# A spectral tokenizer and a transformer block: the first pass's order, the last pass rewritten with four banks for fc1, and head rows that are not turned

## The chip, the cores and the metric

The kernel runs on one core of a Trainium2 chip. All data are 32-bit floats. The metric is the device time of one execution in microseconds; the median of three runs is given. The profile is of one more execution.

## The reference, cut to what matters

For 128 images of 64x64 pixels with 3 channels a Fourier network with 32 channels makes one number per pixel; the 64x64 numbers of an image are then 64 tokens of width 64 for one transformer block.

```python
h = layer_norm(x @ fc0_w + fc0_b, ln0_g, ln0_b)
for i in range(4):
    h = spectral_conv(h, w1, w2) + conv(h) + conv_b[i]      # 24 x 12 modes are kept
    h = layer_norm(h, ln_g[i], ln_b[i])
    if i < 3: h = gelu(h)
h = gelu(h @ fc1_w + fc1_b)          # 32 -> 128
h = gelu(h @ fc2_w + fc2_b)          # 128 -> 64
h = h @ fc3_w + fc3_b                # 64 -> 1, "the head"
h = concatenate([cls_tok, h])        # 65 tokens of width 64
h = h + state_space_scan(layernorm(h))
h = h + (attention, then 8 experts of which 2 are chosen)(layernorm(h))
```

## The kernel before, in words

The program has two parts, `build_tokenizer` and `build_block`, one after the other with a barrier between. In each part every engine has a program of its own, in an order written by hand, and engines meet at counting semaphores.

**Tokenizer.** It makes five passes over the images, and between two passes mixes the Fourier modes of a layer. A pass takes two images (a pair) per step, 64 steps, in a loop that does two steps a turn (`p` is 0 or 1, which buffer). A step handles 4 chunks `j` of 512 columns. The chunk numbers run through all passes; `g0` is the first chunk of the step, and `behind(...)` names the chunk that a stage works on `lag` chunks later, so one step holds the front of its own pair and the back of the one before.

- In a pass PE forms a chunk in a bank `H` (first pass: `inverse_y`, L313, from the turned image `image_t`; later passes: `conv` plus `inverse_y`), ACT squares it (`squares`), DVE sums the squares (`variance`), POOL raises to the power -1/2 (`pool_step`, L683), and DVE multiplies (`normal`; in the first four passes three operations, with gain and shift). ACT then writes the chunk twice (`gelus`, L383 and L387), PE turns it to channels (`to_channels`, L325), ACT copies that out (`channels_out`, L393), and `forward_x` (L337) and `forward_y` (L347) make the spectrum. `pe_mid`, `act_mid` and `dve_mid` are the programs of the first four passes.
- First and middle passes had the same order before: chunks go in twos (`inverse_y(0)`, `inverse_y(1)`, later 2 and 3; the same for `squares` and `variance`).
- The last pass (`pe_last`, `act_last`, `dve_last`) has the three dense layers in place of the spectrum. The activations lie as 4 row groups of 32 channels; `fc1` (`dense1_of`, L524) multiplies each group with a 32x128 weight. Two matmuls go to the banks `M[0]` and `M[1]`, ACT reads them with a GELU (L600), and then the other two go to the same banks. `fc2` (`dense2_of`, L531) writes two halves of `TP`, then two of `H[3]`, which ACT reads (L606). `fc3` (`dense3_of`, L543) takes two chunks and writes 4 column groups of `H[2]`; DVE copies it (L648), PE turns the copy with 4 transposes (`turn_heads`, L551), DVE adds the bias and picks columns (L658), and SP stores 64 numbers per partition (L252). Gain and shift of the last norm are applied by ACT while it copies from the turned bank `TC` (L593). The spectrum's first inverse step, `inverse_x` (L480), writes `M[0]` and `M[1]`, and ACT copies each to `v_sb` (L613).

**Block.** 16 groups of 8 images. `scan_phase(g, g-1)` runs the scan of a group beside the experts of the one before, `attention_phase(g)` follows. SP loads the tokens of a group into `rows` (L1291) when the group before has turned its own; PE turns them with 4 matmuls (L1382), DVE copies the result to `h_in` (L1645) and puts the class token beside it (L1647), and the first norm begins (`mean` on PE, L1339, then `cen` on DVE, L1581).

## Time and profile before

| | |
|---|---|
| median of 3 runs | 9224.98 us (9206.96 to 9254.56) |
| the profiled execution's own time | 9221.47 us |
| its span | 9219.4 us |
| busy: PE, DVE, ACT, POOL | 7821.1 (85%), 4927.3 (53%), 5171.0 (56%), 4060.8 (44%) us |
| granted TensorE clock, mean over the span | 0.898 |

### The profile page before, as it was taken

How to read it: one execution, taken by the hardware profiler on the slowest of the kernel's cores; microseconds unless marked ns; L12 is line 12 of the kernel's file. 1: busy time of each engine (PE TensorE's matmuls, PEld its weight loads, DVE VectorE, ACT ScalarE, POOL GpSimd, SP SyncE). 2: the span in 40 equal slices, each digit the busy share in tenths (PEclk: the TensorE clock that was granted, in tenths of full speed). 3: DMA queues.
4: the chain of work that ended last, by engine and by line, in shares of the span. 5: the costliest groups of instructions: out<-in, count | busy, mean ns of one | idle time of the engine just before them, and what ended most of it. 6: DMA issues, size and time to landing. Idle time of an engine off the chain costs nothing. (4 is left out here: it accounts for less than half of the span.)

```text
span 9219.4 us, 151061 instructions
## 1 busy us (share of the span) xinstructions
PE 7821.1 (85%) x50544; PEld 5411.4 (59%) x50544; DVE 4927.3 (53%) x8481; ACT 5171.0 (56%) x8851; POOL 4060.8 (44%) x1780
## 2 busy tenths in 40 slices
PE   7778789998899988999889999999967676767767
PEld 4555467776677766777654444444436455555555
DVE  5666657776577765777622222222245555555554
ACT  5676657776577765777656666666632222121212
POOL 6676537776377763777523333333321111111110
PEclk7887799999999989999999999999978787878787
DMA  1121244444444444444431111111100000000000
GB/s 67 75 79 74 83 164 160 154 157 137 169 158 150 158 136 173 153 157 157 142 112 38 38 38 42 38 38 38 38 31 2 2 2 2 2 1 2 1 2 1
DMA packets 569388, 730.82 MB, mean 79 GB/s; under 512 B 451944, under 2 KB 490984, under 8 KB 503656
## 3 DMA queue, kind: packets, MB, share of 16 engines
q1 hardware_dynamic: 569320, 729.87, 24.0%
q8 instruction: 48, 0.79, 0.0%
q14 instruction: 20, 0.16, 0.0%
HBM read 375.30 MB, written 354.45 MB: 79 GB/s over the span
## 5 line engine op out<-in xcount | busy, mean ns | idle before, releaser
L683 POOL TENSOR_TENSOR sb_rstd<-sb_var,sb_minus_half 128x16 f32<-128x16 f32 x1280 | 3697.4, 2903 | 3052.9 <-DVE sb_var L427 1599.3
L337 PEld LDWEIGHTS M<-sb_table,sb_pix 128*128 128x128 f32 x8192 | 1024.9, 206 | 196.3 <-ACT sb_pix L387 132.9
L387 ACT ACTIVATE sb_pix<-sb_unit 128x512 f32<-128x512 f32 x1024 | 1101.8, 1076 | 0.0
L434 DVE TENSOR_TENSOR sb_unit<-H,sb_rstd 128x512 f32<-128x512 f32 x1024 | 703.0, 687 | 682.9 <-POOL sb_rstd L683 677.5
L337 PE MATMUL M<-sb_table,sb_pix 128*128 128x52 f32 x8192 | 1041.2, 289 | 0.0
L383 ACT ACTIVATE sb_act_px<-sb_unit 128x512 f32<-128x512 f32 x1024 | 646.9, 632 | 582.0 <-DVE sb_unit L440 581.3
L325 PE MATMUL TC<-sb_table,sb_act_px 128*128 128x128 f32 x4096 | 688.2, 294 | 227.3 <-ACT sb_act_out L393 114.3
L1812 POOL TENSOR_TENSOR blk_dB<-blk_dB,blk_dB 128x260 f32<-128x260 f32 x256 | 187.4, 735 | 1462.3 <-DVE blk_dB L1672 1457.1
L427 DVE TENSOR_REDUCE sb_var<-sb_square 128x16 f32<-128x528 f32 x1024 | 672.2, 696 | 287.8 <-ACT sb_square L376 287.7
L304 PE MATMUL H<-sb_conv_block,sb_act_in 128*128 128x128 f32 x6144 | 780.6, 281 | 0.0
L325 PEld LDWEIGHTS TC<-sb_table,sb_act_px 128*128 128x128 f32 x4096 | 499.4, 154 | 461.8 <-issue 334.2
L304 PEld LDWEIGHTS H<-sb_conv_block,sb_act_in 128*128 128x128 f32 x6144 | 727.4, 194 | 38.6 <-issue 24.6
L600 ACT ACTIVATE sb_dense<-M,sb_fc_bias 128x512 f32<-128x512 f32 x1024 | 647.4, 683 | 178.5 <-PE M L524 178.5
L437 DVE TENSOR_TENSOR sb_unit<-sb_unit,sb_gain_row 128x512 f32<-128x512 f32 x1024 | 708.5, 692 | 35.1
L440 DVE TENSOR_TENSOR sb_unit<-sb_unit,sb_shift_row 128x512 f32<-128x512 f32 x1024 | 708.5, 692 | 34.9
L376 ACT ACTIVATE sb_square<-H 128x512 f32<-128x512 f32 x1024 | 562.0, 594 | 233.7 <-PE H L318 124.2
L524 PE MATMUL M<-sb_act_out,sb_fc_rep 32*128 32x512 f32 x2048 | 677.1, 640 | 3.2 <-ACT sb_dense L600 2.3
L393 ACT ACTIVATE sb_act_out<-TC 128x512 f32<-128x512 f32 x1024 | 611.4, 597 | 44.8 <-PE TC L325 43.9
L1514 ACT ACTIVATE blk_silu<-bank 114x260 f32<-114x260 f32 x384 | 148.7, 387 | 858.6 <-PE bank L1356 856.4
L636 DVE TENSOR_REDUCE sb_var<-sb_square 128x16 f32<-128x528 f32 x256 | 179.9, 703 | 740.8 <-ACT sb_square L587 740.8
L1396 PE MATMUL bank<-blk_bc,blk_select 128*128 128x260 f32 x1536 | 446.2, 406 | 113.6 <-DVE blk_dB L1686 85.3
L524 PEld LDWEIGHTS M<-sb_act_out,sb_fc_rep 32*128 32x128 f32 x2048 | 226.4, 183 | 440.8 <-ACT sb_dense L600 207.7
(231 smaller groups left out, 12102.2 us busy)
## 6 DMA issues: line engine op xcount, KB each, us to landing
act_scratch<-sb_act_out SPq DMA_DIRECT2D x256, 1024.0 KB, 3.9
sb_act_in<-act_scratch SPq DMA_DIRECT2D x256, 1024.0 KB, 5.3
spectrum_in<-sb_f_sb SPq DMA_DIRECT2D x512, 78.0 KB, 1.8
sb_x_in<-spectrum_in SPq DMA_DIRECT2D x48, 832.0 KB, 4.2
spectrum_out<-sb_y_sb SPq DMA_DIRECT2D x48, 832.0 KB, 4.4
sb_z_in<-spectrum_out SPq DMA_DIRECT2D x512, 78.0 KB, 5.1
sb_w_raw<-in_w_mix_dram SPq DMA_DIRECT2D x48, 208.0 KB, 4.0
sb_image_in<-in_x_dram SPq DMA_DIRECT2D x64, 96.0 KB, 2.0
```

What stands on the lines that cost most here:

```text
L304: e.matmul(H[j][:, 128 * u:128 * u + 128], act_in[p][:, 128 * b:128 * b + 128], conv_block[:, :], start=(u == 0), stop=False, skip_group_c ...
L325: mm = e.transpose(TC[:, 128 * u:128 * u + 128], act_px[k % 2][:, 128 * u:128 * u + 128], const("ident"))
L337: mm = e.matmul(M[u][:, 52 * g:52 * g + 52], pix[1 - p][:, at:at + 128], const("f1"), start=True, stop=True)
L383: e.activation(act_px[k % 2][:, :], unit[k % 2][:, :], gelu).then_inc(px_ready, 1)
L387: e.activation(dst, unit[k % 2][:, :].rearrange("p (x c) -> p c x", c=16), gelu).then_inc(pix_ready, 1)
L427: e.tensor_reduce(var[j][:, :], square[j % 2][:, :].rearrange("p (y c) -> p y c", c=C + 1), AX.X, ALU.add).then_inc(var_ready, 1)
L434: e.tensor_tensor(rows, H[k][:, :].rearrange("p (y c) -> p y c", c=C), rstd[k][:, :].unsqueeze(2).to_broadcast([128, 16, C]), ALU.mult).th ...
L437: e.tensor_tensor(rows, rows, gain_row[:, :].unsqueeze(1).to_broadcast([128, 16, C]), ALU.mult).then_inc(scaled, 1)
L440: e.tensor_tensor(rows, rows, shift_row[:, :].unsqueeze(1).to_broadcast([128, 16, C]), ALU.add).then_inc(affine_ready, 1)
L524: e.matmul(M[v][:, :], fc1_rep[at:at + 32, :], act_out[q][at:at + 32, 512 * k:512 * k + 512], start=True, stop=True).then_inc(fc1_done, 1)
L600: e.activation(dense1[2 * w + v][:, :], M[v][:, :], ACT.Gelu, bias=fc1_bias[:, 0:1], scale=1.0).then_inc(fc1_act, 1)
L683: e.tensor_tensor(rstd[j][:, :], var[j][:, :], minus_half[:, :], ALU.pow).then_inc(rstd_ready, 1)
```

## The change

- First pass only: PE, ACT and DVE take the chunks one at a time. `inverse_y(j+1)` stands behind each `to_channels`, `squares(j+1)` and `gelus` alternate, and DVE alternates `variance` and `normal`. The middle passes keep their order.
- Last pass: new programs for PE, ACT and DVE. `fc1` writes four banks (`M[0]`, `M[1]`, `TP`, `H[3]`) from its four row groups at once; `fc2` then writes two of them. `inverse_x` uses `H[2]`, one half after the other, in turn with `fc3`. Gain and shift are folded into `fc1` ahead of the pass (`fc1_scaled`, `fc1_shifted`), and DVE, not ACT, copies `TC` out. `turn_heads` and the two small DVE operations go: DVE adds the bias as it copies `H[2]` to `head_rows`, and SP stores rows of 512 numbers, 4 DMAs per pair in place of 1.
- Block: since the heads now lie in DRAM image by image, 32 DMAs per group write `h_in` itself, 4 partitions each. The loads of group `g+1` are issued once `h1` of group `g` is there. The turning matmuls and both DVE copies go; the class token is written once.

```diff
-                e.dma_start(heads[n], head[p][:, :]).then_inc(st_h[p], 16)
+                for half in range(2):
+                    e.wait_ge(head_ready, 2 * n + half + 1)
+                    for v in range(2):
+                        e.dma_start(heads[n][half, v], head_rows[half][v:128:32, :]).then_inc(st_h[half], 16)
                 return
...
                 if front and not first and j % 2 == 0:
                     conv(j)
                     conv(j + 1)
+                if front and first and j == 0:
+                    inverse_y(0)
                 if three:
                     to_channels(*three)
-                if front and j % 2 == 0:
+                if front and first and j < 3:
+                    inverse_y(j + 1)
+                if front and not first and j % 2 == 0:
                     inverse_y(j)
                     inverse_y(j + 1)
...
             for j in range(4):
                 two, three = (behind(g0, p, j, lag, front, back) for lag in (2, 3))
-                if two and j == 0:
+                if front and first and j == 0:
+                    squares(0)
+                if two and (first or j == 0):
                     gelus(*two)
                 if three:
                     channels_out(*three)
-                if front and j % 2 == 0:
+                if front and first and j < 3:
+                    squares(j + 1)
+                if front and not first and j % 2 == 0:
                     squares(j)
                     squares(j + 1)
-                if two and j > 0:
+                if two and not first and j > 0:
                     gelus(*two)
...
+            if first:
+                for j in range(4):
+                    if front:
+                        variance(j)
+                    if front and j > 0:
+                        normal(g0 + j - 1, j - 1)
+                    if back and j == 0:
+                        normal(g0 - 1, 3)
+                if back:
+                    spectrum()
+                return
...
+        FC1 = (M[0], M[1], TP, H[3])
...
+            def dense1_of(c, q, k):
+                e.wait_ge(act_ready, c + 1)
+                at_least(e, fc2_act, 2 * (c - HEAD0))
+                for r in range(4):
+                    e.matmul(FC1[r][:, :], fc1_scaled[32 * r:32 * r + 32, :],
+                             act_out[q][32 * r:32 * r + 32, 512 * k:512 * k + 512],
                              start=True, stop=True).then_inc(fc1_done, 1)
+            def dense2_of(c):
+                for w in range(2):
+                    e.wait_ge(fc1_act, 4 * (c - HEAD0) + 2 * w + 2)
+                    for v in range(2):
+                        mm = e.matmul(FC1[w][64 * v:64 * v + 64, :], fc2_w[:, :], dense1[2 * w + v][:, :],
+                                      start=True, stop=True, skip_group_check=True)
+                    mm.then_inc(fc2_done, 1)
...
+            if front:
+                inverse_x(0)
+            if back:
+                dense1_of(g0 - 4, 1 - p, 0)
+                to_channels(g0 - 3, 1)
+            if front:
+                inverse_x(1)
+            if back2:
+                if front:
+                    e.wait_ge(v_ready, 2 * it + 2)
+                else:
+                    e.wait_ge(head_ready, 2 * local - 3)
+                dense3_of(g0 - 5)
+            if back:
+                dense2_of(g0 - 4)
+            if front:
+                conv(0)
+            if back:
+                dense1_of(g0 - 3, 1 - p, 1)
+            if front:
+                conv(1)
+            if back:
+                to_channels(g0 - 2, 2)
+            if front:
+                inverse_y(0)
+                inverse_y(1)
+            if back:
+                dense2_of(g0 - 3)
+                to_channels(g0 - 1, 3)
+                dense1_of(g0 - 2, 1 - p, 2)
+                at_least(e, head_ready, 2 * local - 2)
+                dense3_of(g0 - 3)
+                dense2_of(g0 - 2)
+            if front:
+                conv(2)
+            if back:
+                dense1_of(g0 - 1, 1 - p, 3)
+            if front:
+                conv(3)
+                to_channels(g0, 0)
+                inverse_y(2)
+                inverse_y(3)
+            if back:
+                dense2_of(g0 - 1)
+            if not front:
+                e.wait_ge(head_ready, 2 * local - 1)
+                dense3_of(g0 - 1)
...
+                intermediate(0)
+            if back:
+                dense1_of(g0 - 4)
+            if front:
+                intermediate(1)
+            if back:
+                dense2_of(g0 - 4, 0)
+                dense1_of(g0 - 3)
+            if front:
+                squares(0)
+                squares(1)
+            if back:
+                dense2_of(g0 - 3, 1)
+                dense1_of(g0 - 2)
+                dense2_of(g0 - 2, 2)
+                dense1_of(g0 - 1)
+            if front:
+                squares(2)
+                squares(3)
+            if back:
+                dense2_of(g0 - 1, 3)
...
+            def channels_out(c, q, k):
+                e.wait_ge(tc_ready, c + 1)
+                e.tensor_copy(act_out[q][:, 512 * k:512 * k + 512], TC[:, :]).then_inc(act_ready, 1)
+            def copy_heads(half, ago):
+                e.wait_ge(fc3_done, 2 * (local - ago) + half + 1)
+                at_least(e, st_h[half], 32 * (local - ago))
+                e.tensor_scalar(head_rows[half][:, :], H[2][:, :], fc3_bias[:, 0:1], None,
+                                ALU.add).then_inc(head_ready, 1)
+            if back:
+                channels_out(g0 - 3, 1 - p, 1)
+                normal(g0 - 2, 2)
+            if back2:
+                copy_heads(1, 2)
+            if back:
+                normal(g0 - 1, 3)
+                channels_out(g0 - 2, 1 - p, 2)
+            if front:
+                variance(0)
+                variance(1)
+            if back:
+                channels_out(g0 - 1, 1 - p, 3)
+                copy_heads(0, 1)
+            if front:
+                normal(g0, 0)
+                normal(g0 + 1, 1)
+                channels_out(g0, p, 0)
+                variance(2)
+                variance(3)
+            else:
+                copy_heads(1, 1)
...
+                    e.tensor_scalar(fc1_scaled[:, :], fc1_rep[:, :], gain[:, 0:1], None, ALU.mult).then_inc(fold_set, 1)
+                    e.wait_ge(fold_pe, 1)
+                    e.tensor_tensor(fc1_shifted[:, :], TC[:, 0:1], fc1_bias[:, :], ALU.add).then_inc(fold_set, 1)
...
-                e.dma_start(rows[:, :].rearrange("x (m y) -> x m y", m=GI), h0_rows[g]).then_inc(rows_in, 16)
+                for i in range(2):
+                    for a in range(4):
+                        for u in range(4):
+                            at = D * i + 16 * a + 4 * u
+                            e.dma_start(by_token(h_in[at:at + 4, :])[:, :, 1:T], h0_rows[g][a, u, i]).then_inc(rows_in, 16)
...
-            wait(e, "rows_t", 0)
+            wait(e, "h1", 0)
             load(1)
             with e.Fori(1, groups - 1) as g:
+                wait(e, "h1", g)
                 store(g - 1)
                 e.wait_ge(stored, 16 * g)
...
-                e.wait_ge(rows_in, 16 * (g + 1))
-                for q in range(Q):
-                    mm = e.matmul(B[0][:, T * q + 1:T * q + T], rows[:, 128 * q:128 * q + 128],
-                                  const("ident")[0:S, 0:S], start=True, stop=True, skip_group_check=True)
-                mm.then_inc(sig["rows_t"], 1)
-                wait(e, "h_in", g)
+                e.wait_ge(rows_in, 512 * (g + 1))
...
-                wait(e, "rows_t", g)
-                e.tensor_copy(by_token(h_in[:, :])[:, :, 1:T], by_token(B[0][:, 0:TOK])[:, :, 1:T])\
-                    .then_inc(sig["h_in"], 1)
-                e.tensor_copy(by_token(h_in[:, :])[:, :, 0:1], wt("cls").unsqueeze(1).to_broadcast([128, Q, 1]))\
-                    .then_inc(sig["h_in"], 1)
-                wait(e, "h_in", g)
```

PE in the first pass, one step. Before (`H` are the four chunk banks, `TC` the turned bank, `M` takes `forward_x`):

```order
L325 MATMUL TC<-sb_table,sb_act_px 128x128 x4
L310 ISA
L313 MATMUL H<-sb_fc_block,sb_image_t 128x512 x2
L322 REGISTER_ALU
L325 MATMUL TC<-sb_table,sb_act_px 128x128 x8
L313 MATMUL H<-sb_fc_block,sb_image_t 128x512 x2
L337 MATMUL M<-sb_table,sb_pix 128x52 x16
```

And now:

```order
L317 MATMUL H<-sb_fc_block,sb_image_t 128x512
L326 REGISTER_ALU
L329 MATMUL TC<-sb_table,sb_act_px 128x128 x4
L317 MATMUL H<-sb_fc_block,sb_image_t 128x512
L326 REGISTER_ALU
L329 MATMUL TC<-sb_table,sb_act_px 128x128 x4
L317 MATMUL H<-sb_fc_block,sb_image_t 128x512
L329 MATMUL TC<-sb_table,sb_act_px 128x128 x4
L317 MATMUL H<-sb_fc_block,sb_image_t 128x512
L341 MATMUL M<-sb_table,sb_pix 128x52 x16
```

The four matmuls that form the chunks stood in twos; now one stands between each two turns.

PE in the last pass, fc1 of one chunk and its neighbours (L524 is fc1, L502 `inverse_y`, L509 `to_channels`, L531 fc2). Before:

```order
L531 MATMUL H3<-sb_dense1_3,sb_fc2_w 64x512
...
L524 MATMUL M0<-sb_act_out1,sb_fc1_rep 128x512
L524 MATMUL M1<-sb_act_out1,sb_fc1_rep 128x512
L502 MATMUL H0<-sb_v_sb,sb_table 128x512
L502 MATMUL H1<-sb_v_sb,sb_table 128x512
L225 REGISTER_ALU
L524 MATMUL M0<-sb_act_out1,sb_fc1_rep 128x512
L225 REGISTER_ALU
L524 MATMUL M1<-sb_act_out1,sb_fc1_rep 128x512
L509 MATMUL TC<-sb_table,sb_unit0 128x128 x4
L531 MATMUL TP<-sb_dense1_0,sb_fc2_w 64x512
```

Now (L540 is fc1, L516 `conv`, L531 `to_channels`, L524 `inverse_y`, L548 fc2):

```order
L516 MATMUL H0<-sb_conv_block,sb_act_in0 128x128 x4
L226 ISA
L540 MATMUL M0<-sb_act_out1,sb_fc1_scaled 128x512
L540 MATMUL M1<-sb_act_out1,sb_fc1_scaled 128x512
L540 MATMUL TP<-sb_act_out1,sb_fc1_scaled 128x512
L540 MATMUL H3<-sb_act_out1,sb_fc1_scaled 128x512
L516 MATMUL H1<-sb_conv_block,sb_act_in0 128x128 x4
L531 MATMUL TC<-sb_table,sb_unit0 128x128 x4
L524 MATMUL H0<-sb_v_sb,sb_table 128x512
L524 MATMUL H1<-sb_v_sb,sb_table 128x512
```

The two halves of fc1 stood apart, the second behind a wait for the banks of the first; now the four matmuls stand together.

PE at the start of a step of the last pass, now (L503 is `inverse_x`, L556 fc3), up to fc2:

```order
L503 MATMUL H2<-sb_table,sb_z_in0 52x128 x8
L570 REGISTER_ALU
L554 ISA
L556 MATMUL H2<-sb_dense2_0,sb_fc3_pad 32x512
L556 MATMUL H2<-sb_dense2_1,sb_fc3_pad 32x512
L556 MATMUL H2<-sb_dense2_2,sb_fc3_pad 32x512
L556 MATMUL H2<-sb_dense2_3,sb_fc3_pad 32x512
L546 ISA
L548 MATMUL M0<-sb_dense1_0,sb_fc2_w 64x512
```

Before, `inverse_x` had banks of its own; now fc3 waits behind it for the same bank, which ACT has to copy out first.

## Rows read from the trace of the kernel before

**Rows 1.** Busy time by stretch: first, middle, last pass, block (us, busy by engine, PEclk, DMA).

```profile
20.00:1110.00 1090.00, 865.89 (x3899) 567.56 (x3899) 712.28 (x1080) 739.06 (x1265) 739.03 (x255) 0.80 0.20 75
1300.00:2200.00 900.00, 846.57 (x7196) 681.02 (x7194) 653.33 (x987) 710.32 (x1162) 668.50 (x233) 0.97 0.48 156
4800.00:6700.00 1900.00, 1856.81 (x10424) 840.54 (x10420) 444.81 (x829) 1271.64 (x2019) 687.09 (x237) 1.00 0.14 39
7000.00:9100.00 2100.00, 1470.78 (x8049) 1157.19 (x8047) 1183.22 (x2505) 442.22 (x1022) 317.78 (x434) 0.80 0.01 2
```

**Rows 2.** One line's instructions: first matmuls of a step, first pass, then last pass.

```profile
L285 PE MATMUL M<-sb_table,sb_image_in x128: 272/313/449, 18.8 to 1095.4; 128*96 128x128 f32 x128
...
L480 PE MATMUL M<-sb_table,sb_z_in x2048: 272/273/452, 4699.9 to 6719.5; 96*52 96x128 f32 x187
```

**Rows 3.** Timeline of PE, last pass (start, us, engine, line, op, count, idle before).

```profile
5215.35 1.08 PE L531 MATMUL H<-sb_dense,sb_fc_w 128*64 128x512 f32 x4
5216.35 1.13 PE L524 MATMUL M<-sb_act_out,sb_fc_rep 32*128 32x512 f32 x4
5217.41 1.13 PE L502 MATMUL H<-sb_v_sb,sb_table 52*128 52x512 f32 x4
5218.47 1.48 PE L524 MATMUL M<-sb_act_out,sb_fc_rep 32*128 32x512 f32 x4
5219.88 0.65 PE L509 MATMUL TC<-sb_table,sb_unit 128*128 128x128 f32 x4
5220.47 1.08 PE L531 MATMUL TP<-sb_dense,sb_fc_w 128*64 128x512 f32 x4
5221.38 1.03 PE L531 MATMUL H<-sb_dense,sb_fc_w 128*64 128x512 f32 x4
...
5223.39 1.06 PE L543 MATMUL H<-sb_dense,sb_fc_pad 128*32 128x512 f32 x8
...
5227.46 0.66 PE L551 MATMUL H<-sb_table,sb_head_rows 128*128 128x128 f32 x4
...
5229.74 1.16 PE L494 MATMUL H<-sb_conv_block,sb_act_in 128*128 128x128 f32 x8 [0.73 <-DVE sb_unit L642]
```

**Rows 4.** Timeline of ACT, last pass, same step.

```profile
5217.51 1.26 ACT L600 ACTIVATE sb_dense<-M,sb_fc_bias 128x512 f32<-128x512 f32 x2 [0.35 <-PE M L524]
...
5220.78 0.78 ACT L593 ACTIVATE sb_act_out<-TC,sb_shift,sb_gain 128x512 f32<-128x512 f32 x1
5221.59 0.69 ACT L606 ACTIVATE sb_dense<-TP,sb_fc_bias 128x512 f32<-128x512 f32 x1
```

**Rows 5.** Timeline of POOL, first pass: after a step at low clock, after one at full.

```profile
241.33 11.53 POOL L683 TENSOR_TENSOR sb_rstd<-sb_var,sb_minus_half 128x16 f32<-128x16 f32 x4 [9.24 <-DVE sb_var L427]
...
1023.76 11.53 POOL L683 TENSOR_TENSOR sb_rstd<-sb_var,sb_minus_half 128x16 f32<-128x16 f32 x4 [3.23 <-DVE sb_var L427]
```

**Rows 6.** Timeline of PE, first pass, before and after the clock fell at 1025.

```profile
1019.37 1.98 PE L313 MATMUL H<-sb_fc_block,sb_image_t 97*128 97x512 f32 x4 [0.57 <-ACT sb_image_t L399]
...
1024.49 0.83 PE L325 MATMUL TC<-sb_table,sb_act_px 128*128 128x128 f32 x4 [1.25 <-ACT sb_act_px L383]
1025.12 3.44 PE L313 MATMUL H<-sb_fc_block,sb_image_t 97*128 97x512 f32 x4
```

**Rows 7.** Timeline of all engines, block, end of one group's attention phase.

```profile
7201.52 1.97 PE L1382 MATMUL bank<-blk_tables,blk_rows 64*128 64x64 f32 x8
...
7207.71 0.42 DVE L1645 COPY blk_h_in<-bank 128x256 f32<-128x256 f32 x1 [0.53 <-DVE blk_lg L1796]
...
7208.27 1.23 PE L1339 MATMUL bank<-blk_h_in,blk_tables 128*128 128x260 f32 x2 [4.78 <-DVE blk_h_in L1647]
7209.53 0.43 DVE L1581 TENSOR_TENSOR blk_cen<-blk_h_in,bank 128x260 f32<-128x260 f32 x1 [1.33 <-PE bank L1339]
```

**Rows 8.** Timeline of SP's queue, block, then last pass.

```profile
7154.88 0.64 SPq L1291 DMA_DIRECT2D blk_rows<-tokens  x1
...
5212.14 0.36 SPq L252 DMA_DIRECT2D tokens<-sb_head  x1
```

277 lines of the change are left out of this document (93 added, 184 removed).

## Prediction

> **What bounds the kernel now.** I read the busy time by stretch first. The first pass runs at a granted clock of 0.80 with no engine full: PE 866 of 1090 us, POOL 739, ACT 739 [rows 1]. The middle passes are PE's (847 of 900 us, clock 0.97), and so is the last pass, at 1857 of 1900 us and a clock of 1.00 [rows 1]. The block fills no engine, a chain of small operations. Then the length of a step, from the first and last start of the matmuls that open one: 128 transposes, two per step, from 18.8 to 1095.4 us, so (1095.4 - 18.8) / 63 = 17.1 us in the first pass; in the last pass (6719.5 - 4699.9) / 63 = 32.06 us [rows 2]. Both passes have 64 steps. The rest is read from timelines of one step.
>
> **The last pass: PE's work.** In PE's stream I take the distance between starts. The first half of fc1 costs 5217.41 - 5216.35 = 1.06 us, the second 5219.88 - 5218.47 = 1.41, because its matmuls wait until ACT has read the banks [rows 3]; in ACT's rows the two GELUs take 1.26 us [rows 4]. Per step that is 4 x (1.06 + 1.41) = 9.9 us. Now the four row groups go together.
> - No row shows four row groups at once. Lower bound: fc3 runs eight records in four column groups in 1.06 us [rows 3]. Upper bound: two halves without a wait, 2.12. I take 1.28, near the lower one: the four are as independent as fc3's, but each loads weights 128 wide, not 32, and I give the two additional loads 0.11 us each. So fc1 costs 5.1 per step, 4.8 less.
> - The head turns go. From the turn's start to the next convolution that cost about 0.5 us, twice a step [rows 3]: 1.0 less.
> - The second pair of convolutions waited 0.73 us for `normal`, once a step [rows 3]. The new order takes the convolutions apart; 0.7 less.
> - fc2 behind fc2 costs 5221.38 - 5220.47 = 0.91 us, and followed by fc1 5216.35 - 5215.35 = 1.00 [rows 3]. All four now have their halves together, before two had: 0.2 less.
>
> Sum: 32.06 - 4.8 - 1.0 - 0.7 - 0.2 = 25.4 us of work per step.
>
> What I just called 0.09 us is a change of tile shape. The Trainium skill ("TensorEngine Tiling (Array Packing)", section Tiling Modes, Key Properties) says that changing the tiling mode drains the engine. By my count of the order, a step had 26 such changes and now has 19. By that rule, at the 0.09 us of the row, 0.4 us more than I count goes, and the pass would be 27 us shorter again.
>
> **The last pass: new waits.** There is one set of fc1 banks now, and each chunk waits for it. From the rows: fc1's start to its first GELU 5217.51 - 5216.35 = 1.16 us, four GELUs 2 x 1.26 = 2.5, fc2's start to its GELU 5221.59 - 5220.47 = 1.12, that GELU 0.69 [rows 3, 4].
> - fc3 at the head of a step waits for both copies of `inverse_x`. The second is queued on ACT behind four GELUs: 1.16 + 2.5 + 0.7 = 4.4 us after fc1's start, while PE has 1.3 + 0.6 + 0.9 = 2.8 us to do. 1.5 us of waiting. DVE waits there too, in `copy_heads`, with `normal` queued behind it; those units are needed two stages later.
> - In the third chunk only fc3 stands between fc1 and fc2: the second half of fc2 needs all four GELUs, 3.7 us, and PE has 1.3 + 1.06 + 1.0. 0.4 us.
> - The next fc1 needs both GELUs of fc2: 1.12 + 0.69 = 1.8 after fc2's second half starts. Where only a turn (0.6) lies between, 0.3 us; elsewhere a convolution covers it.
> - The rest, semaphores between four engines, 0.2.
>
> That is 2.4, so a step takes **27.8 us**, and the pass is 64 x 4.3 = **275 us** shorter. ACT is no bound: 16 GELUs at 0.63, 8 at 0.69, and 6 copies and squares at 0.6 are 19 us, after the 0.78 us copy of each chunk went to DVE [rows 4], which is busy 445 of 1900 us [rows 1]. SP issues three more stores per step, at 0.36 us each [rows 8], in a step of 28 us. Were PE all work, 25.4, the gain would be 426 us: that is the upper end.
>
> **The block.** The first norm began when DVE, done with the gates, had copied at 7207.71; then `mean` on PE, and `cen` at 9.53. Now `mean` needs nothing of DVE and is done under the gates, where the turn stood at 7201.52 [rows 7], so `cen` can stand at 7207.71: 1.8 us per group, 15 groups, **27 us**. Cover: 32 loads at up to the 0.64 us of one load now [rows 8] are 20 us of issue, from 7154.88, against 53 us until they are needed. Without that cover it would cost up to 20 us, which is what the first group can lose; it has the block's set-up beside it, and I count 0. Ends: -27 and +20.
>
> **The first pass.** At the full clock a step takes 11.53 + 3.23 = 14.8 us, at the low clock 11.53 + 9.24 = 20.8 [rows 5]. I see no shorter ring in the new order: POOL's four operations stay in one chain with ACT's writes, and it still waits between steps. What can change is the clock. Before one fall PE had one group of turns between 1021.35 and 1024.49; the pairs of L313 then took 3.44 us instead of 1.98, the level of 1.2 GHz [rows 6]. The new order puts one 0.94 us chunk matmul between the turns, so that this quiet stretch is cut, but walked through with the rows' durations it also leaves three gaps of over 1 us per step where there were two. Ends: all steps at 14.8, a gain of 64 x 2.3 = 149 us; all at 20.8, a loss of 237. I take a third of the gain, **45 us**, since the total of PE's work per step stays.
>
> **Sum.** 9221.5 - 275 - 27 - 45 = 8874 for the profiled execution; the median of the runs stands 3.5 above it, and I forecast 8875.
>
> **Rivals.**
> 1. *The four row groups run two by two.* For it: all row-group matmuls in the trace come in twos. Against: fc3 shows four column groups at once [rows 3]. Then fc1 costs 2.12 and a step 3.4 us more, of which 0.7 fills the second and third wait: +2.7 x 64 = 170 us, 9045. The Trainium skill ("TensorEngine Tiling (Array Packing)", section Overview, Theoretical Speedup) gives up to 4x for a dimension of 32 or less; by that rule this rival falls. Chance 0.10.
> 2. *The single set of banks makes a longer chain than counted.* One chunk's ring is 3.7 + 1.12 + 0.69 = 5.5 us, 22 per step, with fc1 to fc1 through ACT; each copy or square that lands inside it adds 0.6. With all six inside it and PE's fragments beside, 1 us more per chunk: 31.8 per step, 9130. Against: the order puts most of them where PE works on something else. Chance 0.08.
> 3. *The first pass keeps the full clock throughout.* -104 more: 8770. For it: falls follow quiet stretches. Chance 0.15.
> 4. *Slower: the clock falls in the last pass.* It held 1.00 at 98% busy; at 94% it was 0.97, at 79% 0.80 [rows 1]. With 25.4 in 27.8 PE is at 91%. At the low level work doubles, 25 us per step. The gain of 347 us is gone once 14 of 64 steps are low, a granted clock of 0.89; at the 0.86 of 18 steps the time is 8875 + 450 = 9325. Against: the two busy shares bracket it near 0.96, which would cost some 100 us and is in my range. Chance 0.04.
> 5. *The first pass loses,* its clock near the low level: up to +282, 9155. Chance 0.04.
>
> The forecast case has 0.59. Within 0.5% (46 us, about what a measurement of this kernel can tell from no change) I put 0.02, a mild form of the fourth rival; slower is 0.03, the rest of it and the fifth together with worse waits; faster is what is left, 0.95. The range takes in a first pass at the full clock with somewhat smaller waits, and below it the pairs of rival 1 or a part of rival 2: 8730 to 9020.
>
> **What would show it.** In the last pass: a distance between starts of `inverse_x` of 27.8 us; fc1's eight records within 1.3 us from start to the next instruction; PE idle some 1.5 us ahead of fc3 with ACT's `v_sb` as releaser; a clock of 0.96 or more. In the first pass: a step of 16.4 us, 14.8 at the full clock, and a granted clock of 0.85. In the block: a group 1.8 us shorter, `cen` right behind the last gate. I am wrong if fc1 takes 2.1 us, if ACT's GELUs leave no gap, or if the last pass shows a clock under 0.9.

## The result, and the profile after

| | before | after |
|---|---|---|
| median of the runs | 9215.97 us (4 runs, 9198.99 to 9254.56) | 8868.56 us (4 runs, 8838.37 to 8874.36) |
| the profiled execution | 9221.47, span 9219.4 | 8874.36, span 8872.5 |
| busy PE, DVE, ACT, POOL | 7821, 4927, 5171, 4061 us | 7376.5, 5045.7, 4957.5, 4051.4 us |
| granted clock | 0.898 | 0.893 |

The ratio is 0.9616, with a 95% interval of 0.9587 to 0.9646: faster, by 347 us. The forecast of 8875 is met to the microsecond by the profiled execution, and within 7 us by the median. That is luck: the terms of the sum were wrong in both directions. The same views as before the change show it. First the stretches: first pass, last pass, block (length, busy time of PE, PEld, DVE, ACT, POOL, granted clock, DMA share, GB/s).

```profile
20.00:1110.00 1090.00, 865.12 (x3848) 567.87 (x3848) 707.33 (x1064) 716.96 (x1245) 723.43 (x252) 0.79 0.20 74
4700.00:6420.00 1720.00, 1577.00 (x10680) 723.88 (x10680) 596.76 (x891) 1156.59 (x1901) 737.45 (x256) 0.99 0.17 46
6460.00:8872.50 2412.50, 1678.79 (x9086) 1304.47 (x9086) 1346.05 (x2831) 505.25 (x1168) 363.19 (x496) 0.79 0.01 3
```

Then the opening matmuls of a step, in the first pass (L289) and the last (L503; the last fields but one are the first and the last start).

```profile
L289 PE MATMUL M<-sb_table,sb_image_in x128: 272/315/450, 18.6 to 1111.8; 128*96 128x128 f32 x128
L503 PE MATMUL H<-sb_table,sb_z_in x2048: 270/273/457, 4705.5 to 6391.4; 96*52 96x128 f32 x187
```

A step of the first pass takes (1111.8 - 18.6) / 63 = 17.35 us, against 17.09 [rows 2]: 16 us lost where I had forecast 45 gained. A step of the last pass takes (6391.4 - 4705.5) / 63 = 26.76 us, against 32.06: 5.3 less per step, 334 us over 63 steps, where I had forecast 4.3 and 275. The last pass begins 5.6 us later than before (4705.5, 4699.9), so 11 us of the first pass's loss came back between the two. From the start of its last step to the block's first `cen` 68.1 us pass instead of 75.7, and from there to the end of the span 2413.0 instead of 2424.2. The account: +5.6 - 333.7 - 7.6 - 11.2 = -346.9 us, the difference of the spans.

The 26.76 us are a mean of two kinds of step, as the first matmul of fc3 shows in three steps that follow each other:

```profile
4874.63 1.07 PE L556 MATMUL H<-sb_dense,sb_fc_pad 128*32 128x512 f32 x8
...
4902.94 1.06 PE L556 MATMUL H<-sb_dense,sb_fc_pad 128*32 128x512 f32 x8
...
4929.61 1.06 PE L556 MATMUL H<-sb_dense,sb_fc_pad 128*32 128x512 f32 x8
```

Nearly all steps take 4929.61 - 4902.94 = 26.67 us. Six take 28.31, as the one ahead of it did; in those the granted clock was 0.50 for a short stretch.

One step of the last pass on PE, rows picked (fc1 is L540, fc2 L548, fc3 L556, `inverse_x` L503; x4 is two matmuls):

```profile
5046.35 1.05 PE L503 MATMUL H<-sb_table,sb_z_in 96*52 96x128 f32 x16
5047.33 0.70 PE L540 MATMUL M<-sb_act_out,sb_fc_scaled 32*128 32x512 f32 x2
5047.34 0.69 PE L540 MATMUL TP<-sb_act_out,sb_fc_scaled 32*128 32x512 f32 x1
5047.35 0.69 PE L540 MATMUL H<-sb_act_out,sb_fc_scaled 32*128 32x512 f32 x1
...
5048.40 0.66 PE L531 MATMUL TC<-sb_table,sb_unit 128*128 128x128 f32 x4
5048.98 1.08 PE L503 MATMUL H<-sb_table,sb_z_in 96*52 96x128 f32 x16
5051.54 1.07 PE L556 MATMUL H<-sb_dense,sb_fc_pad 128*32 128x512 f32 x8 [1.47 <-ACT sb_v_sb L616]
...
5061.87 0.70 PE L540 MATMUL M<-sb_act_out,sb_fc_scaled 32*128 32x512 f32 x2 [0.20 <-ACT sb_dense L635]
...
5064.35 2.23 PE L548 MATMUL M<-sb_dense,sb_fc_w 128*64 128x512 f32 x8 [0.34 <-ACT sb_dense L629]
```

The four matmuls of fc1 start within 0.02 us of each other, and the next instruction starts 5048.40 - 5047.33 = 1.07 us after the first: the lower bound of my term, not the 1.28 that I took. Against 2.47 for the two halves before [rows 3]. The three waits stand where they were expected, at 1.47, 0.34 and 0.20 us (1.5, 0.4 and 0.3 forecast). Beside the first, on ACT, the copy of `v_sb` stands behind four GELUs:

```profile
5048.49 1.26 ACT L629 ACTIVATE sb_dense<-M,sb_fc_shifted 128x512 f32<-128x512 f32 x2 [0.45 <-PE H L540]
5049.64 0.69 ACT L629 ACTIVATE sb_dense<-TP,sb_fc_shifted 128x512 f32<-128x512 f32 x1
5050.21 0.70 ACT L629 ACTIVATE sb_dense<-H,sb_fc_shifted 128x512 f32<-128x512 f32 x1
5050.78 0.61 ACT L616 ACTIVATE sb_v_sb<-H 116x512 f32<-116x512 f32 x1
```

In the block, DVE's timeline at the end of a group. The last gate (L1824) and `cen` (L1615) are 6869.98 - 6869.22 = 0.76 us apart. Before, the last gate (L1796) stood at 7206.95 and `cen` at 7209.53 [rows 7], 2.58 us apart. The 1.8 us are there, at each of the 15 boundaries. The block as a whole shows 11, not 27. The first row is from before the change, the other two from after it.

```profile
7206.95 0.22 DVE L1796 TENSOR_TENSOR blk_lg<-blk_lg,blk_st 65x64 f32<-65x64 f32 x1
...
6869.22 0.22 DVE L1824 TENSOR_TENSOR blk_lg<-blk_lg,blk_st 65x64 f32<-65x64 f32 x1
6869.98 0.43 DVE L1615 TENSOR_TENSOR blk_cen<-blk_h_in,bank 128x260 f32<-128x260 f32 x1 [0.55 <-DVE blk_lg L1824]
```

So I had two open questions: where the block's 16 us and the first pass's 45 went, and whether fc1's gain is what the last pass lives on.

### The profile page after: what moved, and what is told of

It is laid out like the page before. It is cut to its first block and busy times, and to the rows that moved or that the text cites. A ratio compares the mean times of both kernels' runs of the same rounds, so it can differ in the third digit from the quotient of the medians.

```text
span 8872.5 us, 151116 instructions
## 1 busy us (share of the span) xinstructions
PE 7376.5 (83%) x49906; PEld 5199.5 (59%) x49906; DVE 5045.7 (57%) x8452; ACT 4957.5 (56%) x8595; POOL 4051.4 (46%) x1780
## 5 line engine op out<-in xcount | busy, mean ns | idle before, releaser
L341 PEld LDWEIGHTS M<-sb_table,sb_pix 128*128 128x128 f32 x8192 | 1047.1, 210 | 189.9 <-ACT sb_pix L395 124.2
L341 PE MATMUL M<-sb_table,sb_pix 128*128 128x52 f32 x8192 | 1065.4, 294 | 0.0
L439 DVE TENSOR_REDUCE sb_var<-sb_square 128x16 f32<-128x528 f32 x1024 | 681.0, 696 | 425.4 <-ACT sb_square L384 425.4
L680 DVE COPY sb_act_out<-TC 128x512 f32<-128x512 f32 x256 | 177.0, 691 | 649.2 <-PE TC L531 649.2
L548 PE MATMUL M<-sb_dense,sb_fc_w 128*64 128x512 f32 x2048 | 516.2, 614 | 28.7 <-ACT sb_dense L629 23.7
L629 ACT ACTIVATE sb_dense<-M,sb_fc_shifted 128x512 f32<-128x512 f32 x512 | 323.8, 683 | 291.2 <-PE H L540 291.2
L295 PEld LDWEIGHTS M<-sb_table,sb_z_in 96*52 96x52 f32 x6144 | 395.3, 140 | 134.6 <-issue 133.5
```

Of the source, the lines that this page charges most:

```text
L341: mm = e.matmul(M[u][:, 52 * g:52 * g + 52], pix[1 - p][:, at:at + 128], const("f1"), start=True, stop=True)
L439: e.tensor_reduce(var[j][:, :], square[j % 2][:, :].rearrange("p (y c) -> p y c", c=C + 1), AX.X, ALU.add).then_inc(var_ready, 1)
```

## Experiments

The figures of each kernel are the median and the ratio to the kernel before, run on the same chip; 0.001 of ratio is 9 us. The ratio of the changed kernel is 0.9616.

**The first pass's order, taken out and alone.** The first kernel is the changed one with PE, ACT and DVE of the first pass in the old order, the second the kernel before with the new one. The cut shows PE's part of the first; ACT's and DVE's part go back in the same way.

```diff
-                if front and first and j == 0:
-                    inverse_y(0)
                 if three:
                     to_channels(*three)
-                if front and first and j < 3:
-                    inverse_y(j + 1)
-                if front and not first and j % 2 == 0:
+                if front and j % 2 == 0:
                     inverse_y(j)
                     inverse_y(j + 1)
```

> The changed kernel with the first pass's order put back (chunks in twos), all else as changed. Between the two traces the first pass went from 17.1 to 17.35 us per step, 16 us in all, where I had forecast a gain of 45. Theory A: the new order itself costs this, through a granted clock that stays at 0.79 and POOL's chain that is no shorter: with the old order the first pass is back at 17.1 per step and the whole is 10 to 20 us shorter, near 8857. Theory B: the order makes no difference and the 16 us are chance of where the clock falls in one execution: the time is that of the changed kernel, within 5 us, and the step anywhere between 17.0 and 17.4.

> The kernel before with nothing but the first pass's new order. Theory A (the order costs): a first pass of 17.3 to 17.4 us per step, the whole 10 to 20 us slower than the kernel before, near 9230. Theory B (chance): within 5 us of the kernel before. My forecast, already in doubt, had 45 us of gain here, a step of 16.4.

Measured: 8876.38 us, ratio 0.9605 (0.9582 to 0.9628), and 9233.63 us, ratio 0.9998 (0.9979 to 1.0016). Neither can be told from no change; the second excludes a gain of over 19 us, and so my 45, and a loss of over 15. The opening matmuls of the first pass with the old order:

```profile
L289 PE MATMUL M<-sb_table,sb_image_in x128: 272/313/449, 18.3 to 1081.8; 128*96 128x128 f32 x128
```

And with the new order in the kernel before:

```profile
L285 PE MATMUL M<-sb_table,sb_image_in x128: 272/368/450, 18.6 to 1127.8; 128*96 128x128 f32 x128
```

The steps are 16.88 us (old order, granted clock 0.82 between 20 and 1110 us) and 17.61 (new order, 0.77). The other traces with the new order and nothing added in this pass, from the runs below, have 17.1 to 17.4 us. In the traces the new order looks some 0.3 us per step slower, on two traces of the old one; the times don't settle it.

**The four row groups.** The third and fourth matmul of fc1 use the rows of the first and second again, so this kernel leaves out half of fc1's products and computes the other half twice.

```diff
                 for r in range(4):
-                    e.matmul(FC1[r][:, :], fc1_scaled[32 * r:32 * r + 32, :],
-                             act_out[q][32 * r:32 * r + 32, 512 * k:512 * k + 512],
+                    i = 32 * (r % 2)
+                    e.matmul(FC1[r][:, :], fc1_scaled[i:i + 32, :],
+                             act_out[q][i:i + 32, 512 * k:512 * k + 512],
```

> The changed kernel, but fc1's third and fourth matmul take rows 0 to 63 of weights and activations again (so half of fc1's outputs repeat the other half's), which puts them on the row groups that the first two still use. Banks, waits and instruction counts stay. Theory A: the four row groups work at the same time, and that is what the four banks bring on PE: fc1 now needs 2.1 us where the changed kernel's rows show 1.07, that is 4.2 us more per step, of which 0.5 to 0.7 fills the waits ahead of the third chunk's fc2; step 30.3 us, some 225 us more, near 9095. Rival: the row groups make no difference, what counts is that no wait stands between the pairs: fc1 stays at 1.07 to 1.3 and the time within 20 us.

Measured: 8983.00 us, ratio 0.9728 (0.9706 to 0.9751), 103 us more by the ratios. A chunk on PE and its wait:

```profile
5052.51 1.13 PE L541 MATMUL M<-sb_act_out,sb_fc_scaled 32*128 32x512 f32 x4
5053.47 0.59 PE L541 MATMUL TP<-sb_act_out,sb_fc_scaled 32*128 32x512 f32 x1
...
5054.43 0.66 PE L531 MATMUL TC<-sb_table,sb_unit 128*128 128x128 f32 x4
5055.01 1.08 PE L503 MATMUL H<-sb_table,sb_z_in 96*52 96x128 f32 x16
5056.88 1.06 PE L557 MATMUL H<-sb_dense,sb_fc_pad 128*32 128x512 f32 x8 [0.79 <-ACT sb_v_sb L617]
```

The second pair starts 0.96 us after the first (5053.47, 5052.51) and fc1 costs 1.92 us, so row groups that differ do run at once, four as well as two: theory A in kind. In size it was too dear. Of 4 x 0.85 = 3.4 us more per step 2.0 arrive (nearly every step takes 28.66 us, against 26.67). The waits ahead of fc3 (1.47 to 0.79) and of the third fc2 (0.34 to nothing) take 1.0, and the third fc2 itself, in which the second half waits too, gets 0.3 shorter. What the rival of pairs would have cost was 103 us, not 170.

**Two banks for fc1.** The four row groups again, but the second pair writes the first pair's banks, as before the change, and fc2 goes to `TP` and `H[3]`. ACT's reads follow in the same way.

```diff
                 for r in range(4):
-                    e.matmul(FC1[r][:, :], fc1_scaled[32 * r:32 * r + 32, :],
+                    if r == 2:
+                        e.wait_ge(fc1_act, 4 * (c - HEAD0) + 2)
+                    e.matmul(FC1[r % 2][:, :], fc1_scaled[32 * r:32 * r + 32, :],
...
-                        mm = e.matmul(FC1[w][64 * v:64 * v + 64, :], fc2_w[:, :], dense1[2 * w + v][:, :],
+                        mm = e.matmul(FC1[2 + w][64 * v:64 * v + 64, :], fc2_w[:, :], dense1[2 * w + v][:, :],
```

> The changed kernel with two banks for fc1, as before: its third and fourth matmul write M[0] and M[1] again and wait for ACT's first two GELUs; fc2 writes TP and H[3]. Theory A: the four banks are what the new order stands on. The first pair takes 1.07, the first GELU starts 1.16 after it and the two take 1.26, so the second pair starts 2.42 after the first and fc1 costs PE 3.5 instead of 1.07, as nothing stands between the pairs here: 9.7 us more per step, less the 1.5 + 0.3 + 0.2 of waits that it fills: about 7.7, step 34.5, 490 us more, near 9360, slower than the kernel before. Rival: part of it is hidden; then 3 to 5 us per step, 9060 to 9190.

Measured: 9963.82 us, ratio 1.0772 (1.0735 to 1.0810), twice the loss of theory A. Two rows of PE, each two matmuls of fc1:

```profile
5042.50 1.13 PE L542 MATMUL M<-sb_act_out,sb_fc_scaled 32*128 32x512 f32 x4
5044.97 1.13 PE L542 MATMUL M<-sb_act_out,sb_fc_scaled 32*128 32x512 f32 x4 [1.35 <-ACT sb_dense L631]
```

The stretch from 4800 to 6000 us of the last pass:

```profile
4800.00:6000.00 1200.00, 1023.22 (x4626) 425.40 (x4624) 255.55 (x386) 520.64 (x828) 317.09 (x110) 0.79 0.10 29
```

The second pair starts 2.47 us after the first, as worked out (2.42). But the step is 43.6 us, not 34.5, because the granted clock is now 0.79 in this stretch (0.78 over the whole pass) where it was 0.99. What PE did otherwise is nearly the same; new are four waits of 1.35 us per step, and PE stands idle 6.4 us of a step where it stood 2.0. This is the fourth rival of the prediction, in another kernel: new waits on PE in the last pass are paid twice, once as waits and once through the clock.

**The copy of `v_sb` earlier.** PE's second `inverse_x` goes ahead of a turn, and ACT copies it after two GELUs.

```diff
                 dense1_of(g0 - 4, 1 - p, 0)
-                to_channels(g0 - 3, 1)
             if front:
                 inverse_x(1)
+            if back:
+                to_channels(g0 - 3, 1)
...
-                dense1_of(g0 - 4)
+                dense1_of(g0 - 4, range(0, 2))
             if front:
                 intermediate(1)
             if back:
+                dense1_of(g0 - 4, range(2, 4))
```

> The changed kernel with PE's inverse_x(1) ahead of the turn of chunk g0-3 and with ACT's copy of it between the second and the third GELU of fc1. In the changed kernel's trace PE waits 1.47 us per step ahead of fc3, until ACT, behind four GELUs, has copied v_sb. Theory A: this wait is a matter of the place in ACT's queue: it falls to about 0.3 us, nothing else gets longer, and the last pass is 64 x 1.15 = 74 us shorter, near 8795. Theory B: the ring through the single set of fc1 banks and ACT sets the step, so that the time comes back as waits ahead of fc2 and fc1 (0.34 and 0.20 now): under 25 us of gain, with these two waits longer by 0.8 together.

Measured: 8776.51 us, ratio 0.9505 (0.9482 to 0.9528), 102 us less by the ratios. PE ahead of fc3:

```profile
5071.33 1.07 PE L556 MATMUL H<-sb_dense,sb_fc_pad 128*32 128x512 f32 x8 [0.32 <-ACT sb_v_sb L617]
```

The opening matmuls of the last pass:

```profile
L503 PE MATMUL H<-sb_table,sb_z_in x2048: 270/273/455, 4690.1 to 6295.0; 96*52 96x128 f32 x187
```

The step is 25.47 us, 1.29 less, of which the wait gives 1.15 (26.67 to 25.52 in nearly every step); the waits at fc2 and fc1 are unchanged at 0.34 and 0.20. The rest is mostly the clock: the six longer steps of the changed kernel are gone. Theory A holds: the place in ACT's queue was the cause, and no ring behind it takes the gain back. The pass gives 82 us of the 102.

**A pause in the block.** Four additions on DVE between the last gate and `cen`.

```diff
+                if k == 0:
+                    for to in pause:
+                        e.tensor_tensor(to[:, :], tables[:, 0:TOK], tables[:, TOK:2 * TOK], ALU.add)
                 if k < 2:
                     wait(e, "mean", g, k + 1)
```

> The changed kernel with four additions on DVE (128x260, into tiles that nobody reads) between the last gate of a group and cen, about 1.85 us, as long as what the change took away there. In the traces the step from the last gate to cen went from 2.58 to 0.76 us, but the groups of the changed kernel are 148.1 to 150.15 us apart, before 150.1 to 150.2, and with the old first pass 150.18 in most groups: the rest of a group grew by up to 1.8 us, in 0.53 us jumps at matmul pairs. Theory A: the granted clock, which changes at other places of the group when the start moves, gives the gain back: the pause costs 0.4 to 0.6 us per group, groups 150.2, the block 6 to 12 us longer. Rival: the gain is real and something else ate it (the 32 loads per group): the pause costs its full 1.85 us, groups of 151.6 us, 28 us in all.

Measured: 8875.07 us, ratio 0.9624 (0.9600 to 0.9648), 7 us more, which the times can't tell from no change. So the traces have to answer. DVE at a boundary:

```profile
7011.62 1.45 DVE L1616 TENSOR_TENSOR blk_pause<-blk_tables 128x260 f32<-128x260 f32 x4 [0.51 <-DVE blk_lg L1828]
7012.99 0.42 DVE L1619 TENSOR_TENSOR blk_cen<-blk_h_in,bank 128x260 f32<-128x260 f32 x1
```

The pause was 1.37 us, not 1.85. The first and the last `cen` of the 16 groups, first in the changed kernel, then with the pause:

```profile
L1615 DVE TENSOR_TENSOR blk_cen<-blk_h_in,bank x16: 424/426/427, 6459.5 to 8663.2; 128x260 f32<-128x260 f32 x16
L1619 DVE TENSOR_TENSOR blk_cen<-blk_h_in,bank x16: 415/418/426, 6449.8 to 8664.9; 128x260 f32<-128x260 f32 x16
```

The groups are (8664.9 - 6449.8) / 15 = 147.7 us apart, against 146.9 in the changed kernel: 0.77 us of the 1.37, 11 us in 15 groups where the full length would be 21. The five other traces with the same block, from this section, have 146.8 to 147.2; the two with the old block have 147.6 and 147.8. Where the rest goes can be read within the changed kernel itself. Two of its groups, 148.05 and 150.14 us long, start alike; at the second norm, on PE:

```profile
6963.13 0.71 PE L1376 MATMUL bank<-blk_h,blk_tables 128*128 128x260 f32 x2 [1.18 <-DVE blk_h L1723]
6964.88 0.73 PE L1378 MATMUL bank<-blk_sqr,blk_tables 128*128 128x260 f32 x2 [1.04 <-ACT blk_sqr L1534]
...
7112.25 1.23 PE L1376 MATMUL bank<-blk_h,blk_tables 128*128 128x260 f32 x2 [1.18 <-DVE blk_h L1723]
7114.52 1.24 PE L1378 MATMUL bank<-blk_sqr,blk_tables 128*128 128x260 f32 x2 [1.04 <-ACT blk_sqr L1534]
```

Same matmuls, 0.71 and 1.23 us: the two levels of the clock. In the long group the clock has fallen ahead of this place, in the short one only behind it. Four delays of 0.5 to 0.6 us, the two here and two at operations some 60 us into the group, make up the 2.1 us between the groups. Before the change nearly every group was 150.1 to 150.2 us apart, after it they are 148.1, 149.7 or 150.1. So the change took 1.8 us off each boundary, and the stretches at 1.2 GHz, which now fall elsewhere in the group, gave back about 1 on average. The 32 loads do not hold up `cen`, since it follows the last gate; what else they might delay was not tested.

**Idle matmuls in the first pass.** Nothing that anyone reads, only work for PE where it waited.

```diff
+            def warm(bank, n):
+                for _ in range(n):
+                    e.matmul(bank[:, 0:96], const("ident"), const("ident")[:, 0:96], start=True, stop=True)
...
+                if j == 0 and first:
+                    at_least(e, unit_ready, g0 - 3)
+                    warm(H[0], 5)
...
                     inverse_y(j + 1)
+                    if j < 2:
+                        warm(M[0], (7, 7)[j])
```

> The changed kernel with idle matmuls in the first pass alone (ident on 96 of its columns, 5 ahead of the first chunk of a step into H[0], 7 each behind the second and third into M[0]), where PE waits 1.1 to 1.5 us at three places of a step; some 0.16 us each at the full clock, so 0.8 to 1.1 us per place. Theory A (the clock, not the order of chunks, sets the first pass): the granted clock rises from 0.79 to above 0.9 and the step falls from 17.35 toward the 14.8 us of a step at the full clock, 100 to 160 us less. Rival: the clock falls all the same, and at 1.2 GHz the 19 matmuls take 6 us of a step in which PE has no room, so the pass is longer by 60 to 200 us.

Measured: 8706.51 us, ratio 0.9434 (0.9411 to 0.9457), 168 us less by the ratios. For comparison, PE in a step of the changed kernel at the full clock:

```profile
442.27 1.02 PE L317 MATMUL H<-sb_fc_block,sb_image_t 97*128 97x512 f32 x2 [1.25 <-ACT sb_image_t L407]
...
446.11 0.63 PE L329 MATMUL TC<-sb_table,sb_act_px 128*128 128x128 f32 x4 [1.52 <-ACT sb_act_out L401]
...
449.04 0.63 PE L329 MATMUL TC<-sb_table,sb_act_px 128*128 128x128 f32 x4 [1.44 <-ACT sb_act_out L401]
```

These waits are what is filled. The first 900 us of the filled kernel:

```profile
20.00:900.00 880.00, 868.34 (x5899) 679.77 (x5898) 668.12 (x1006) 675.21 (x1180) 684.49 (x238) 1.00 0.23 86
```

Its opening matmuls:

```profile
L289 PE MATMUL M<-sb_table,sb_image_in x128: 272/293/421, 18.2 to 951.1; 128*96 128x128 f32 x128
```

The clock is 1.00 and the step 14.81 us, the 14.8 that the rows had for a step at the full clock [rows 5]. Theory A: the clock is what the first pass is short of. It falls with PE waiting three times a step, 1.1 to 1.5 us each, and busy 79% of the time; with these waits filled it stays. The Trainium skill ("TensorE: Matmul & The Clock Gate", section HAM oscillation — how this bites in real kernels) describes a matmul kernel in which each tile's work is shorter than the wait for the next DMA, so that the clock falls at every tile, and the remedy there is a loop that keeps PE busy. This trace agrees that waits between pieces of work let the clock fall and that a busy PE keeps it. But the page's waits are some 3 to 5 us long, and in a step of the changed kernel's first pass none is over 1.52.

**Idle matmuls in the block.** The same with `ident` times `ident` of 128 columns.

```diff
+                if k == 0:
+                    warm(B[2], 14)
                 wait(e, "square", g, SQUARED[k] + 1)
                 e.matmul(B[2][:, 0:TOK], const("mean"), sqr[:, :], start=True, stop=True).then_inc(sig["variance"], 1)
+                warm(B[1], (9, 17, 0, 8)[k])
...
+                warm(B[6], 3)
                 wait(e, "q_image", g)
...
                 wait(e, "v_copied", g)
+                warm(B[6], 8)
```

> The changed kernel with idle matmuls in the block alone (ident times ident, 128 columns, some 0.21 us each at the full clock) where PE waits 2 to 8 us for norms, gates, rotated q and the exponentials: 14 before the first variance, 9, 17 and 8 behind the three others, 3 and 8 in the attention. Theory A (the clock costs the block what the change gave it): the granted clock rises from 0.79 toward 1, matmul pairs of 1.24 us become 0.7, and a group falls by 5 to 10 us, 80 to 160 in all. Rival: the clock stays low in these stretches and the idle matmuls delay the work behind them, 0 to 5 us more per group.

Measured: 8831.45 us, ratio 0.9574 (0.9550 to 0.9597), 39 us less by the ratios. From 7000 to 8800 us:

```profile
7000.00:8800.00 1800.00, 1438.96 (x8373) 1187.77 (x8373) 1022.87 (x2159) 386.10 (x892) 272.35 (x372) 0.86 0.01 2
```

The groups are 146.7 to 146.9 us apart but for the first two. Theory A in direction, at half its lower bound: the clock rose from 0.79 only to 0.86, since PE still waited, 3.4 us ahead of the first variance of a group and up to 5.0 in the scan.

**All together.** The early copy, the idle matmuls in the first pass, and more of them in the block; then the same with the old order in the first pass (the first diff above, with 7 idle matmuls behind the first two turns).

```diff
-                    warm(B[2], 14)
+                    warm(B[2], 26)
...
-                warm(B[1], (9, 17, 0, 8)[k])
+                warm(B[1], (13, 24, 0, 8)[k])
...
                     if n == 0:
+                        wait(e, "drive", g, NS - 1)
+                        warm(B[3], 16)
                         wait(e, "drive", g)
...
-                warm(B[6], 3)
+                warm(B[6], 8)
...
-                warm(B[6], 8)
+                warm(B[6], 16)
```

> The early copy of v_sb, the idle matmuls in the first pass, and those in the block together, in the block with more of them where the trace still showed PE waiting at the low clock (26 ahead of the first variance, 13, 24 and 8 behind the variances, 8 and 16 in the attention, 16 ahead of the scan's read-out). The three touch different stages, so their gains against the changed kernel's ratio of 0.9616 should add: 0.0111 (early copy) + 0.0182 (first pass) + 0.0042 (block) = 0.0335, a ratio of 0.928, near 8560; the added matmuls in the block another 0 to 40 us. Rival: the clock does not bear that much work at once or one gain hides another: above 0.935.

> The same with the first pass's old order of chunks and as many idle matmuls, 5 ahead of the first chunk and 7 behind the turns of the first and second quarter of a step. The first pass's orders alone could not be told apart by time (0.9605 and 0.9616, 0.9998 and 1), but in the traces the new one took 17.1 to 17.6 us per step in six, the old one 16.9 and 17.1 in two. Theory A: the orders differ only in what they do to the clock; with the clock held both take 14.8 and the two kernels agree within 10 us. Rival: the new order has a shorter or a longer chain, seen now that the clock no longer blurs it: 0.3 us per step or more, 20 us.

Measured: 8625.14 us, ratio 0.9331 (0.9305 to 0.9358), and 8624.14, ratio 0.9333 (0.9307 to 0.9360). The gains did not add, for a reason in the block, below. The two orders agree within 1 us of median, and in the traces within 3 us over the pass (952.0 and 955.0 for the last opening matmul): with the clock held, the order of chunks is worth nothing. In the block PE's timeline shows, at the start of a group:

```profile
7069.21 1.23 PE L1391 MATMUL bank<-blk_h_in,blk_tables 128*128 128x260 f32 x2 [2.97 <-issue]
...
7072.00 7.83 PE L1386 MATMUL bank<-blk_tables 128*128 128x128 f32 x51 [1.34 <-issue]
7079.66 0.60 PE L1395 MATMUL bank<-blk_sqr,blk_tables 128*128 128x260 f32 x2
```

The idle matmuls run until 7079.66, and the variance (L1395), which had waited 3.4 us for ACT with 14 of them, now waits for them. It starts 7.3 us after `cen`, where 0.93 is usual. That is not the number of idle matmuls alone. The second group of the same trace has the same 26:

```profile
6323.29 5.97 PE L1386 MATMUL bank<-blk_tables 128*128 128x128 f32 x52
6329.67 0.71 PE L1395 MATMUL bank<-blk_sqr,blk_tables 128*128 128x260 f32 x2 [0.41 <-ACT blk_sqr L1556]
```

There PE had no "issue" gap, the idle matmuls were done in time, and the next `cen` came after 142.9 us. From the third group on (the first stands ahead of the loop, the second is its first turn) such gaps, of 2.5 to 3.4 us ahead of `mean` and 1.3 to 1.9 behind it, stand in every group, and the groups take 149.5 to 150.7 us.

**Fewer, and the pause again.** 14 in place of 26 at that point; then this kernel with the pause.

```diff
                 if k == 0:
-                    warm(B[2], 26)
+                    warm(B[2], 14)
```

> The three together again, with 14 idle matmuls ahead of the first variance of a group in place of 26, the rest as in the one before. In that one the groups of the block were 150 us apart, where the fewer idle matmuls alone had given 146.8: PE stood 2.97 us (issue) before the first mean, and the 26 were then not done until 4.9 us after sqr could be there. Theory A: this alone was what the sum lacked: a group 4 to 5 us shorter, 60 to 75 us in all, a ratio of 0.926, near 8555. Rival: with the clock held elsewhere PE gains nothing more in the block: within 15 us of 8625.

> The same kernel with the 1.85 us of DVE additions between the last gate and cen of each group (as in the experiment on the changed kernel, where they cost 0.76 us per group, 11 in all). Theory A: there the falling and rising clock took up the rest; here the granted clock is held through most of a group, so the pause costs more of its length, 1.3 to 1.9 us per group, 20 to 28 in all. Rival: the pause is covered by something other than the clock (a fixed wait of the loop's end or of the 32 loads): again 0 to 0.8 us per group.

Measured: 8522.59 us, ratio 0.9232 (0.9207 to 0.9258), and 8530.42, ratio 0.9251 (0.9226 to 0.9276). The first is the fastest of all, 4% below the changed kernel. From 6600 to 8400 us:

```profile
6600.00:8400.00 1800.00, 1533.71 (x9576) 1294.70 (x9575) 1054.09 (x2212) 398.15 (x923) 293.02 (x400) 0.91 0.01 2
```

Groups are 142 to 146 us apart, at a clock of 0.91. Theory A of the first, if anything too small (92 us by the ratios). But the 12 matmuls fewer also took the "issue" gaps away: in this trace one group has one, where the one with 26 had them in 14, and nearly all of the difference comes with them. Why fewer idle matmuls avoid the gaps stays open. Of the second kernel theory A fell: the pause costs 8 us by the medians, 18 by the ratios, and in the traces nothing (141.6 us from `cen` to `cen` in both). But the rival is not shown either. Laid side by side from `cen`, eight of the 14 full groups run alike for 90 us or more. By the division behind the products with v the kernel with the pause is ahead in most groups, by up to 2.7 us, and there the clock is at 0.50 for 14 to 27 us in both. So the clock is still loose enough there to swallow 1.4 us, and that it does so is likely, but not shown. What a pause would cost with the clock at 1 throughout stays open.

## Why the prediction was right, and where it was not

- **What bounds the kernel**: right. The last pass is PE's, and its gain adds up from PE's rows.
- **fc1**, term -4.8 per step: the mechanism was right and the size off. I added 0.11 us for each additional weight load to the 1.06 of fc3's row; the rows show 1.07, no charge at all. 2.47 - 1.07 over four chunks is -5.6 per step, 54 us more over the pass than the term.
- **Head turns, convolutions, fc2**, -1.9: not separable, but the sum of the step shows them. With fc1 at 1.07 my terms give 25.4 - 0.84 + 2.4 = 27.0 us; measured were 26.76. By the rule on mode changes in the Trainium skill ("TensorEngine Tiling (Array Packing)", section Tiling Modes, Key Properties), 0.4 less would have been due, 26.6. A step at the full clock takes 26.67, but PE's waits were 2.0 us where I had 2.4, so the 0.4 may as well lie there, and the trace bears out neither.
- **New waits**, +2.4: right in place and size (1.47, 0.34, 0.20). What I did not see is that the largest was a matter of the order of two lines on PE and two on ACT, worth 102 us. (My text ahead of the prediction says that `inverse_x` had banks of its own before. It wrote `M[0]` and `M[1]`, a bank for each half, and shared them with fc1.)
- **The block**, -27: the 1.8 us per boundary are there; that they would reach the end was wrong. The term took the rest of a group as fixed, and its clock was not. It gave 11.
- **The first pass**, -45: wrong, and the wrong kind of term. "I take a third of the gain" rested on the walk through the new order's gaps, which counted three over 1 us where there were two, and so spoke against it. Measured: 16 us lost in the trace, nothing that the times can tell. The bounds (149 gained, 237 lost) did hold it, and the filled pass showed the end at -149 to be real.
- **The rivals**: pairs of row groups did not occur, and by the kernel with two groups would have cost 103, not 170, as I let the waits take up too little. The chain of the single bank set did not lengthen. The fourth (the clock falls in the last pass) did not occur at 92% busy, but did at 85% in the kernel with two banks. A straight line between the two busy shares that I used gives 0.95 and 0.87 there; measured were 0.99 and 0.79. For my own 91% it gives 0.94, not the 0.96 that I wrote. And I turned low steps into a granted clock by their number, though it is a mean over time: 14 low steps of 52.8 us among 64 would show as 0.83, not 0.89.

So 59 us too little in the last pass met 61 too much in the first (45 expected, 16 lost) and 16 too much in the block; the rest is the 18 us between the passes and at their ends that I had not counted.

## What to carry to other kernels

Where an engine with two clock levels waits at many short places, read the granted clock by stretch before costing anything, and treat a saving on the chain as worth its length only where the clock is level: 1.8 us saved per group of the block brought 0.75, and a wait added on PE in a full pass cost twice itself. Idle matmuls into a bank that PE owns at that moment are a cheap test of this, and here a gain of 168 us, but look at what they delay: with 26 instead of 14 ahead of one matmul, and the "issue" gaps that came with them, the kernel was 92 us slower. And after a rewrite look first at which queue holds the releaser of the longest new wait; here moving one copy ahead of two GELUs, and one inverse transform ahead of a turn, was worth 102 us more on top of the rewrite's 347.

## What was not expected of the hardware

- Four matmuls on four row groups of 32 rows, each with weights of its own 128 wide and a bank of its own, take 1.07 us, no more than two (1.06 [rows 3]); two pairs on the same row groups take 1.92.
- The granted clock of the last pass was 0.99 with PE busy 92% and waits of up to 1.5 us once per step of 26.8 us, and 0.79 with PE busy 85% and four waits of 1.35 us.
- At the start of a group of the block PE stood up to 3.4 us on "issue", with nothing that it waited for. In the kernel with 26 idle matmuls it did so from the third group on, that is wherever the loop over the groups had turned, and not in the first two. In the changed kernel it did so in no group: `mean` follows the matmul for the gates at once, behind a wait of 3.67 us for the norm. That such a wait covers the gap is a guess that no run tested.
